# Two-layer decoder with routed experts: early blocks fetched in two steps, and eight filler products before the second self-attention

## The reference, cut to what matters

```python
x = x + _L0_attn_ref(_layernorm(x), ...)        # banded self-attention
x = x + _L0_xattn_ref(_layernorm(x), ctx, ctx, ...)
x = x + _L0_ffn_ref(_layernorm(x), ...)         # 8 experts, top 2, hidden 682, gated by silu
x = x + _L1_attn_ref(_layernorm(x), ...)        # full self-attention, 16 heads of 64
x = x + _L1_xattn_ref(ctx, ctx, _layernorm(x), ...)
x = x + _L1_ffn_ref(_layernorm(x), ...)         # 8 experts, top 2, hidden 1024, gelu
```

| after batch | layer 0, expert 0 | layer 0, expert 1 | layer 1, expert 0 | layer 1, expert 1 |
|---|---|---|---|---|
| 2 | 110 | 181 | 200 | 136 |
| 3 | 229 | 247 | 221 | 197 |
| 4 | 366 | 279 | 394 | 199 |
| 7 (all) | 649 | 346 | 713 | 290 |

## Time and profile before

### The profile page before, as it was taken

How to read it: one execution, slowest core, us unless ns; L and a number is a source line. 1 busy time by engine, 2 the same in 40 slices (tenths; PEclk the granted TensorE clock), 3 DMA queues, 4 the chain that set the end, 5 groups by cost and what they waited for, 6 DMA issues and landing times. The chain is left out here.

```text
span 1560.6 us, 34654 instructions
## 1 busy us (share of the span) xinstructions
PE 1455.8 (93%) x11868; PEld 1172.6 (75%) x11869; DVE 744.2 (48%) x2124; ACT 621.6 (40%) x1721; POOL 492.8 (32%) x762
## 2 busy tenths in 40 slices
PE   7999978998999999959999999998799989999996
PEld 5667656767999999936777777776466679999996
DVE  6666646896433333325444444443278952222221
ACT  2333336663122222215445444544266543334332
POOL 4445431444322222213233223323124442222222
PEclk9999998999999999979999999999799989999999
DMA  9910030112243333220000000000301122533331
GB/s 317 333 42 2 2 116 8 36 56 70 52 141 89 90 88 86 34 60 1 1 1 1 1 1 1 1 1 1 114 9 49 53 76 37 145 95 88 96 88 26
DMA packets 80239, 97.82 MB, mean 63 GB/s; under 512 B 10715, under 2 KB 73155, under 8 KB 80131
## 3 DMA queue, kind: packets, MB, share of 16 engines
q1 hardware_dynamic: 65075, 77.98, 15.7%
q0 software_dynamic: 13824, 17.19, 6.4%
q10 hardware_dynamic: 1232, 1.18, 0.2%
HBM read 57.91 MB, written 39.72 MB: 63 GB/s over the span
## 5 line engine op out<-in xcount | busy, mean ns | idle before, releaser
L1496 POOL TENSOR_TENSOR L1a_prob<-L1a_prob,L1a_rtot 128x1024 f32<-128x1024 f32 x64 | 121.1, 1893 | 284.5 <-DVE L1a_rtot L1376 284.5
L1905 PEld LDWEIGHTS L0x_ps<-L0f_rows_t,L0f_w_up 128*128 128x128 f32 x1584 | 183.4, 193 | 12.0 <-issue 10.7
L1905 PE MATMUL L0x_ps<-L0f_rows_t,L0f_w_up 128*128 128x128 f32 x1584 | 185.8, 277 | 6.9 <-issue 4.4
L1973 ACT ACTIVATE L1f_hid<-L1x_ps,L1f_b_up 128x128 f32<-128x128 f32 x304 | 95.0, 363 | 171.7 <-PE L1x_ps L1905 171.7
L1905 PEld LDWEIGHTS L1x_ps<-L1f_rows_t,L1f_w_up 128*128 128x128 f32 x1216 | 143.7, 194 | 4.5 <-issue 2.7
L1905 PE MATMUL L1x_ps<-L1f_rows_t,L1f_w_up 128*128 128x128 f32 x1216 | 145.0, 278 | 1.2 <-ACT L1f_rows_t L1957 1.2
L1914 PE MATMUL L1x_ps<-L1f_w_down,L1f_hid 128*128 128x256 f32 x608 | 137.8, 380 | 2.6 <-DVE L1f_y L2072 2.6
L1441 ACT ACTIVATE L1a_prob<-L1a_ps_s,L1a_nmax 128x256 f32<-128x256 f32 x256 | 118.2, 473 | 40.5 <-DVE L1a_nmax L1371 40.5
L1914 PEld LDWEIGHTS L1x_ps<-L1f_w_down,L1f_hid 128*128 128x128 f32 x608 | 112.7, 190 | 16.7 <-issue 3.0
L1116 POOL TENSOR_SCALAR_AFFINE_SELECT L0a_prob<-L0a_prob 128x128 f32<-128x128 f32 (+1 forms) x256 | 79.7, 353 | 104.5 <-ACT L0a_prob L1084 104.5
L1965 ACT ACTIVATE ctx_in<-L0x_ps 128x256 f32<-128x256 f32 x72 | 27.6, 383 | 187.1 <-PE L0x_ps L1905 187.1
(11 more groups left out here) (386 smaller groups left out, 2765.1 us busy)
## 6 DMA issues: line engine op xcount, KB each, us to landing
expert_table<-zero SPq DMA_DIRECT2D x1, 16640.0 KB, 68.5
L0f_w_up<-in_w_dram SPq DMA_DIRECT2D x8, 1408.0 KB, 6.3
L1f_w_up<-in_w_dram SPq DMA_DIRECT2D x8, 1024.0 KB, 5.0
L1f_w_down<-in_w_dram SPq DMA_DIRECT2D x8, 1024.0 KB, 7.6
L0f_w_down<-in_w_dram SPq DMA_DIRECT2D x8, 768.0 KB, 8.2
L1f_rows<-expert_table SPq DMA_DIRECT2D x36, 130.0 KB, 2.5
L0f_rows<-expert_table SPq DMA_DIRECT2D x34, 130.0 KB
sums<-X SPq DMA_DIRECT2D x8, 256.0 KB, 2.1
```

What stands on the lines that cost most here:

```text
L1496: eng.tensor_tensor(v, v, r.unsqueeze(2).to_broadcast([P, 2 * QT_N, S]), ALU.mult).then_inc(norm_done, 1)
L1905: ins = eng.matmul(ps_h[c][:, o:o + P], w_up[par][:, t, w0:w0 + P], rows_t[:, t, :], start=(t == 0), stop=(t == DT - 1))
L1973: ins = eng.activation(hid[:, c, k * P:(k + 1) * P], ps_h[c][:, k * P:(k + 1) * P], ACT.Gelu, bias=b_up[par][:, 2 * c + k:2 * c + k + 1])
```

## The change

There are three edits. EARLY becomes (0, 0), (1, 0), (0, 1), (1, 1), and SNAPSHOT = 4 becomes FULL_BY = [2, 4]: blocks 0 are compared and fetched when batches 0 to 2 are in the table, blocks 1 when batches 0 to 4 are. Each pair has a semaphore of its own, send(3) waits for the first and send(5) for the second, and PE's and DVE's early steps each wait for the pair that they read. A block 1 counts as full only if it is and its expert's block 0 did: the comparison is multiplied by the flag of block 0. Last, PE makes eight products of `ident` with itself into `ps_o` where `attention_quads` begins, ahead of the first work there.

```diff
@@ -38,6 +38,12 @@
     return (n + 1) * per_block + j + 1
+def idle_products(eng, out, ident, n):
+
+    for _ in range(n):
+        eng.matmul(out[:, 0:P], ident[:, :], ident[:, :], start=True, stop=True)
+
+
 def attention_crossed(nc, name, env, q_scale, wq, wk, wv, wo, bq, bk, bv, bo, w_landed, route, other_loads, experts):
@@ -234,10 +240,11 @@
                     eng.wait_ge(added, b + 1)
                     tiles = slice(b * QT_N, (b + 1) * QT_N)
                     eng.dma_start(route["sums"].rearrange("(t p) d -> p t d", p=P)[:, tiles, :], X[:, tiles, :]).then_inc(route["kept"], 16)
-                    if b == SNAPSHOT + 1:
-                        for par in range(2):
-                            eng.wait_ge(scattered[par], ((SNAPSHOT - par) // 2 + 1) * 64)
-                        experts["load_early"](eng)
+                    for i, last in enumerate(FULL_BY):
+                        if b == last + 1:
+                            for par in range(2):
+                                eng.wait_ge(scattered[par], ((last - par) // 2 + 1) * 64)
+                            experts["load_early"](eng, i)
                 for sc in scattered:
                     eng.wait_ge(sc, B // 2 * 64)
                 experts["sync"](eng)
@@ -389,8 +396,9 @@
                             norm(b + 2)
                         if b >= 3:
                             slots(b - 3)
-                            if b - 3 == SNAPSHOT:
-                                experts["snapshot"](eng)
+                            for i, last in enumerate(FULL_BY):
+                                if b - 3 == last:
+                                    experts["snapshot"](eng, i)
                     else:
                         if b >= 2:
                             choose(b - 2)
@@ -413,7 +421,7 @@
                 x["token_and_gate"](0)
                 add(B - 1)
                 choose(B - 2)
-                x["out"](0, 0)
+                x["out"](0, EARLY[0][0])
                 slots(B - 2)
                 x["hidden"](1, 0)
                 x["hidden"](1, 1)
@@ -425,7 +433,7 @@
                 slots(B - 1)
                 route["list_blocks"](eng)
                 x["token_and_gate"](1)
-                x["out"](1, 0)
+                x["out"](1, EARLY[1][0])
                 for n in range(2, len(EARLY)):
                     for c in range(experts["chunks"]):
                         x["hidden"](n, c)
@@ -610,8 +618,9 @@
                     if b == 0:
                         for s, v in route["zeroed"]:
                             eng.wait_ge(s, v)
-                    if b == SNAPSHOT + 1:
-                        eng.wait_ge(*experts["early_landed"])
+                    for i, last in enumerate(FULL_BY):
+                        if b == last + 1 and tiles[0] == 0:
+                            eng.wait_ge(*experts["early_landed"][i])
                     for q in tiles:
                         for k in range(TOP):
                             eng.indirect_dma_start(route["table"], bass.IndirectOffsetOnAxis(ap=slot_i[:, par, q, k:k + 1], axis=0),
@@ -1590,6 +1599,7 @@
                     if q == QT_N - 1:
                         ins.then_inc(projected, 1)
+                idle_products(eng, ps_o, ident, 8)
                 for e in FIRST:
                     make(0, e)
                 scores(0, 0)
@@ -1663,11 +1673,16 @@
     list_f = tb("list_f", [P, LISTED])
     done = tb("done", [P, EXPERTS + 1])
     link_v, made = nc.alloc_semaphore(f"{name}_link_v"), nc.alloc_semaphore(f"{name}_made")
-    n_early = max(i for _, i in EARLY) + 1
-
-    def snapshot(eng):
+
+    def snapshot(eng, block):
         for k, (e, i) in enumerate(EARLY):
+            if i != block:
+                continue
+            if i:
+                eng.tensor_scalar(full[:, k:k + 1], route["taken"][:, e:e + 1], float((e * REGION + i + 1) * P),
+                                  full[:, EARLY.index((e, i - 1)):EARLY.index((e, i - 1)) + 1], ALU.is_ge, ALU.mult)
+                continue
             eng.tensor_scalar(full[:, k:k + 1], route["taken"][:, e:e + 1], float((e * REGION + i + 1) * P), None, ALU.is_ge)
     full = tb("full", [P, len(EARLY)])
@@ -1684,7 +1699,7 @@
         eng.memset(done[:, :], 0.0)
         linked(eng.tensor_tensor(tokens[:, :], route["taken"][:, :], env["regions"][:, :], ALU.subtract))
-        linked(eng.tensor_reduce(done[:, 0:len(EARLY) // n_early], full[:, :].rearrange("p (e i) -> p e i", i=n_early), AX.X, ALU.add))
+        linked(eng.tensor_reduce(done[:, 0:len(EARLY) // len(FULL_BY)], full[:, :].rearrange("p (i e) -> p e i", i=len(FULL_BY)), AX.X, ALU.add))
         linked(eng.tensor_scalar(blocks_i[:, :], tokens[:, :], float(P - 1), None, ALU.add))
         linked(eng.tensor_scalar(blocks_i[:, :], blocks_i[:, :], 7, None, ALU.logical_shift_right))
         linked(eng.tensor_copy(blocks_f[:, :], blocks_i[:, :]))
@@ -1719,8 +1734,8 @@
-EARLY = [(0, 0), (0, 1), (1, 0), (1, 1)]
-SNAPSHOT = 4
+EARLY = [(0, 0), (1, 0), (0, 1), (1, 1)]
+FULL_BY = [2, 4]
 GATED_FULL = 5
@@ -1776,7 +1791,8 @@
     spare = env["ctx_in"][:, :, :].rearrange("p b d -> p (b d)")
     early_rows = [spare[:, n * ROW:(n + 1) * ROW] for n in range(E)]
-    early_landed = sem("early_landed")
+    early_landed = [sem(f"early_landed{i}") for i in range(len(FULL_BY))]
+    of_block = sum(i == 0 for _, i in EARLY) * 16
     about = tb("about", [P, ROW - D])
     from_end, token = tb("from_end", [P, 1]), tb("token", [P, 1], I32)
     parts, gate = tb("parts", [P, TOP]), tb("gate", [P, 1])
@@ -1814,10 +1830,11 @@
         if after:
             experts(last)
-    def load_early(eng):
+    def load_early(eng, block):
         for n, (e, i) in enumerate(EARLY):
-            first = (e * REGION + i) * P
-            eng.dma_start(early_rows[n][:, :], table[first:first + P, :]).then_inc(early_landed, 16)
+            if i == block:
+                first = (e * REGION + i) * P
+                eng.dma_start(early_rows[n][:, :], table[first:first + P, :]).then_inc(early_landed[i], 16)
     def sync(eng):
         eng.wait_ge(listed["made"], 1)
@@ -1890,7 +1907,7 @@
             ins.then_inc(rows_turned, 1)
         def turn_early(n):
-            eng.wait_ge(early_landed, E * 16)
+            eng.wait_ge(early_landed[EARLY[n][1]], of_block)
             turn(n, early_rows[n])
         def turn_rows(n):
@@ -2094,7 +2111,7 @@
         return dict(start=start, take_early=take_early, hidden=gate_hidden, read_early=read_early,
                     token_and_gate=token_and_gate, out=out_early, rest=rest)
-    return dict(place_banks=place_banks, chunks=CHUNKS, early_landed=(early_landed, E * 16), snapshot=listed["snapshot"], load_early=load_early, sync=sync,
+    return dict(place_banks=place_banks, chunks=CHUNKS, early_landed=[(x, of_block) for x in early_landed], snapshot=listed["snapshot"], load_early=load_early, sync=sync,
                 pool_parts=pool_parts, tensor_parts=tensor_parts, scalar_parts=scalar_parts, vector_parts=vector_parts, sems=used)
```

## The result

The changed kernel was slower, as forecast, but by more: its median was 1592.02 us (1586.2 to 1592.82, 4 runs) against 1574.78 (1572.14 to 1579.59, 4 runs) of the kernel before beside it. The ratio is 1.0099, 95% interval [1.0071, 1.0126], so 11 to 20 us; forecast were 6.9 us and 1581.5, with a range up to 1587.0. The profiled execution took 1586.2 us, with a span of 1584.5 and a clock of 0.974.

The account below looks back on a forecast made before the run. PE, busy 93% of the span, was taken as the bound; 15.4 - 2.9 - 0.7 - 1.7 - 1.9 - 1.3 = +6.9 us gave 1569.2 profiled, 1581.5 us as median with the 12.3 us difference added; range 1576.8 to 1587.0.

Parts of the forecast that it names:

- The early blocks, +15.4: Layer 0's expert 0 fails the earlier judgement, so its two early blocks are made again in the loop: +15.4 us.
- The wait in layer 0, -2.9: Layer 0's tail: PE no longer waits for the early fetch, so `up(0, 0)` begins at 362.6, not 365.5: -2.9 us.
- The next thing to be late is ACT: Layer 0's tail: with the fetch early, ACT's table load and 0.38 us copy set `up(0, 0)`'s start at 362.6.
- The fifth rival: Another step of the chain ends the layers' tails last, so they do not shorten: 1589 us at most; chance 0.04.
- Its clock, -0.7: Layer 0's `up(0, 0)`: half of the 1.4 us to be had if PE's clock stays high: -0.7 us.
- The first rival: Clock stays high at both layers' early blocks and the second self-attention's start: +3.2 us, 1577.8 us; chance 0.12.
- The wait in layer 1, -1.7: Layer 1's tail: without the fetch wait, `up(0, 0)` begins at 1253.0 instead of 1254.72: -1.7 us.
- its clock, -1.9: Layer 1, from `up(0, 0)` on: half of the 3.7 us that low clock cost there: -1.9 us.
- The fillers, -1.3: Start of second self-attention: eight products raise the clock sooner, between +0.4 and -2.5 us, taken as -1.3.
- What is moved and costs nothing: Moved DMAs, send(3)'s wait for the earlier fetch, and DVE's earlier comparisons hold nothing up: no cost.

Follow-up runs that it names:

- e1: The changed kernel run again, unaltered; 1571.75 us, ratio 1.0080 to the kernel before.
- e3: The changed kernel without the eight filler products; 1569.21 us, ratio 1.0060 to the kernel before.
- e2: The changed kernel with blocks 0 judged and fetched after batch 3 instead of 2; 1552.25 us, ratio 0.9953 to the kernel before.
- e4: The kernel before with only the eight filler products added; 1554.69 us, ratio 0.9968 to the kernel before.
- e6: The changed kernel with layer 0's first count of hid given by PE, not DVE's start; 1578.64 us, ratio 1.0044 to the kernel before.
- e10: Repeat on another chip: the changed kernel with layer 0's first count of hid given by PE; 1584.56 us, ratio 1.0051 to the kernel before.
- e11: The changed kernel with blocks 0 judged after batch 3 and layer 0's first count of hid from PE; 1566.01 us, ratio 0.9932 to the kernel before.
- e13: The kernel before with only layer 0's first count of hid given by PE; 1573.32 us, ratio 0.9983 to the kernel before.
- e7: The changed kernel with PE giving the first counts of hid and of rows_ready in both layers; 1580.03 us, ratio 1.0043 to the kernel before.
- e9: The changed kernel again, unaltered, on another chip; 1589.59 us, ratio 1.0085 to the kernel before.
- e14: The changed kernel again, unaltered, on a third chip; 1587.67 us, ratio 1.0073 to the kernel before.

## Why the prediction was wrong in size

- **The early blocks, +15.4: right**, and by its own steps: 38 and 38 adds, eight fetches, 7.72 us each, and the loop longer by 15.4 in e1 and e3 than in e2, e4 and the profile of before. It is why the direction was right.
- **The wait in layer 0, -2.9, is the step that failed**, at "The next thing to be late is ACT". ACT is late next for the turn; for `up(0, 0)` it is DVE, whose `start` gives a count from behind `slots(5)`. The term measured 0 in place of 2.9: the tail changed by 0.4 us at most in four pairs of profiles that have the clock low there for about as long (77.10 to 77.08, 77.12 to 77.14, 86.27 to 85.94, 89.58 to 89.65), with late signals and without. e6, e10 and e11 show it from the other side: with the count from PE, 3.1 to 3.5 us came out of the same stretch in the third group. The row that would have told it, DVE's memset at 365.35, 0.16 us ahead of `up(0, 0)`, was in the trace of before; I took the bracket's ACT for the only releaser of a wait that had two within 0.1 us. Even without DVE the forecast start of 362.6 was 0.6 us too early: it let ACT copy the moment its table load ended, but the turn waited for that load as well, and in the changed kernel's first profile the copy began at 363.14, 0.60 us behind the load's end. The fifth rival had this form ("another step of the chain ends last", 1589 at most), but was given 0.04, on the ground that such a chain would show as a long wait. It did not show because the fetch's wait stood in front of it. (Its 1589 takes the filler's term at -1.3; at that term's own end of +0.4 it would be 1590.4.)
- **Its clock, -0.7: nothing.** PE's idle time around the turn stayed about as long (1.68 and 2.60 us in e1, for 3.78 and 0.68), and the clock was low for 6.8 us there as before: `up(0, 0)` took 3.63 to 3.76 us for its 16 records in every later profile with the count from DVE, and 3.43 in the profile of before. With the count from PE the low stretch at that place was 3.4 us in e6, e10, e11 and e13, and in e7 `up(0, 0)` ran at the high clock (2.02 us), so the shorter gap is worth something, but not all. The first rival, and the rule of the Trainium skill's page "TensorE: Matmul & The Clock Gate" ("HAM oscillation — how this bites in real kernels") beside it, were never put to the test by the change in layer 0, since the waits of PE were only renamed.
- **The wait in layer 1, -1.7, and its clock, -1.9: about a sixth of it.** `up(0, 0)` came 0.85 us earlier, not 1.7, since the sum left out that the turn waits for ACT's table load too (the copy began 0.84 us behind the load's end), and the stretch lost 0.4 to 0.8 us without late signals. The clock was low there for 10.2 us in e1, as in the kernel before, so its term was nothing.
- **The fillers, -1.3: right where they act** (1.3 us; q0 1.99 to 2.00 and k0 1.89 in ten of the twelve profiles with them, q0 3.67 and 3.65 in e7 and e9), though the transposes came 0.67 us late where 0.4 was forecast. What the fillers do to the clock at the end of the stage was in no term.
- **What is moved and costs nothing: right.** The changed kernel's `send(3)` begins at 334.24 behind 4.23 us of waiting for DVE's slots, as in the earlier trace rows, and not for the DMA.

With the measured terms, 15.4 - 0 - 0.6 - 1.3 = 13.5 us, where the three later comparisons gave 11.5 to 12.8. On the base of 1574.6 that is 1588.1, just outside the range. So these terms account for 6.6 of the 10.3 us by which the first measurement (17.2 us by the medians) missed the forecast of 6.9. The first measurement lies in the upper half of its own interval; three of its four runs had a clock of 0.966 or 0.967, where those of e1, e9 and e14 had 0.971 to 0.976 on the mean. That these runs were of that kind by accident is likely by the later groups, but not shown.

The 12.3 us between the profile of before and its median, which I carried over as they stood, are near the 13 us between the group without late signals and those with them. The profile is of an execution without; that the timed runs were of the others is likely, but they have no traces that would show it. It changed no term here, since the tail gained nothing in either.

## What to carry to other kernels

Before a wait is priced, list every semaphore that the waiting instruction needs and find when each was given, also those given by a bare count in another engine's queue; the one that ended last hides the others, and what is won is only the distance to the second (here 0.17 us). A count that needs no work of its engine (a "free at the start") belongs to the engine that waits for it, or ahead of the queue. And an early judgement (full or not) is worth a count over the real data: one batch later cost the tail nothing and saved 15.4 us, and the version with it and the count from PE ran at 0.9932 of the kernel before.

## What was not expected of the hardware

Signals between engines came up to several us late in some executions, or left no record: 93 to 115 instructions in each of 13 profiles, counted as above, and at most one in each of the other five, on the same chip in two groups with and without. In the same 13 profiles over 830 of some 5900 counts by DMAs are missing from the record, in the other five 9 to 15. The kernel before took 1560.5 us in the group whose traces have none and 1573.6 to 1576.0 in the groups whose traces have them, and the step shown above waited 3.9 us in place of 0.85. What brings them on is open. And the same last batch of the self-attention, with no wait in it much over a us, took 39.2 to 45.2 us by where the clock fell, and an edit 400 us ahead of it was worth 5 us alone and nothing to be told in the changed kernel.
